# One decoder layer on one core: context rows summed group by group, finished rows through two PSUM banks, their counts one beat later, the last four groups finished on VectorE

## What is computed

```
x = layernorm(x + mamba(x))
x = layernorm(x + slots(x, ctx))
x = layernorm(x + experts(x))

slots: Pn = rmsnorm(ctx); k, v = Pn @ Wk.T, Pn @ Wv.T
       three times:
         q = rmsnorm(s) @ Wq.T
         a = softmax(q k.T / sqrt(128), over the slots), then divided by its sum over the context
         s = gru(a @ v, s)
experts: route = sigmoid(x @ Wr + br); each row goes to its highest expert e
         out = gelu(x @ W1[e]) @ W2[e] * route[e]
```

## Time and profile before

| | us |
|---|---|
| three runs | 1698.12, 1697.04, 1695.10 (median 1697.04) |
| the profiled execution | 1693.93 |
| its span in the trace | 1691.7 |

### The profile page before, as it was taken

How to read it: one execution, slowest core, us unless ns; L and a number is a source line. 1 busy time by engine, 2 the same in 40 slices (tenths; PEclk the granted TensorE clock), 3 DMA queues, 4 the chain that set the end, 5 groups by cost and what they waited for, 6 DMA issues and landing times. The chain is left out here.

```text
span 1691.7 us, 22066 instructions
## 1 busy us (share of the span) xinstructions
PE 1464.0 (87%) x6146; PEld 892.1 (53%) x6146; DVE 1265.3 (75%) x2184; ACT 1098.0 (65%) x2118; POOL 1264.1 (75%) x884
## 2 busy tenths in 40 slices
PE   4988999999998999899987499999999999419994
PEld 1333344343443334343433377777777777319994
DVE  2899999999999999999993267666766767424552
ACT  4778887788878888778864366656656555104553
POOL 2899999999999999999995144567767666643665
PEclk8999999999999999999998599999999999559997
DMA  5355545554555545554542631421470000026771
GB/s 173 135 193 175 168 166 187 181 176 161 195 173 171 180 162 188 186 185 157 170 152 65 204 125 35 152 99 48 149 306 14 7 8 14 7 81 192 210 207 43
DMA packets 126058, 236.92 MB, mean 140 GB/s; under 512 B 13490, under 2 KB 76917, under 8 KB 125952
## 3 DMA queue, kind: packets, MB, share of 16 engines
q1 hardware_dynamic: 121408, 227.21, 41.3%
q0 software_dynamic: 4544, 8.47, 1.5%
HBM read 180.89 MB, written 55.66 MB: 140 GB/s over the span
## 5 line engine op out<-in xcount | busy, mean ns | idle before, releaser
L388 POOL TENSOR_TENSOR hc<-state,c_rows 128x1024 f32<-128x1024 f32 x256 | 599.1, 2361 | 48.7 <-DVE state L585 39.7
L585 DVE TENSOR_TENSOR_SCAN state<-ps_da,inp 128x512 f32<-128x512 f32 x512 | 592.8, 1203 | 29.5 <-ACT ps_da L481 29.5
L704 PE MATMUL ps_y<-hc,ident 128*128 128x512 f32 x1024 | 491.6, 619 | 53.5 <-POOL hc L388 53.5
L481 ACT ACTIVATE ps_da<-dt,a_neg 128x512 f32<-128x512 f32 x512 | 345.3, 688 | 84.6 <-DVE state L585 83.3
L704 PEld LDWEIGHTS ps_y<-hc,ident 128*128 128x128 f32 x1024 | 194.5, 197 | 295.3 <-issue 211.0
L574 DVE TENSOR_TENSOR inp<-dtx,ps_b 128x1024 f32<-128x1024 f32 x192 | 230.4, 1200 | 37.7 <-POOL dtx L359 22.0
L1047 POOL TENSOR_TENSOR rs<-ms,m_half 128x4 f32<-128x4 f32 x48 | 58.8, 1225 | 164.6 <-DVE ms L1223 164.4
L371 POOL TENSOR_TENSOR inp<-dtx,b_rows 128x1024 f32<-128x1024 f32 x64 | 150.9, 2358 | 0.0
L627 PE MATMUL ps_misc<-x1T,w_conv 128*128 128x512 f32 (+3 forms) x256 | 118.8, 609 | 20.1 <-ACT x1T L414 20.1
L487 ACT COPY ps_b<-b_rows 128x512 f32<-128x512 f32 x192 | 111.1, 579 | 38.1 <-DVE inp L574 35.7
L1156 ACT ACTIVATE ex<-sc,nmx,ctx_r 77x128 f32<-77x128 f32 x192 | 92.3, 482 | 40.3 <-DVE nmx L1236 40.3
(11 more groups left out here) (219 smaller groups left out, 2772.6 us busy)
## 6 DMA issues: line engine op xcount, KB each, us to landing
b_rows<-bc_rows SPq DMA_DIRECT2D x128, 512.0 KB, 4.7
c_rows<-bc_rows SPq DMA_DIRECT2D x128, 512.0 KB, 4.0
sorted_x<-pad_rows SPq DMA_DIRECT2D x8, 4160.0 KB, 16.7
w<-in_L_ffn_W SPq DMA_DIRECT2D x78, 256.0 KB
vw<-vw_rows SPq DMA_DIRECT2D x16, 462.0 KB
vw_rows<-vw_out SPq DMA_DIRECT2D x16, 384.0 KB
xrow<-sorted_x SPq DMA_DIRECT2D x39, 130.0 KB, 2.3
x_tok<-in_x SPq DMA_DIRECT2D x16, 256.0 KB, 4.0
```

The lines of the kernel that those rows point to most:

```text
L388: pool.tensor_tensor(hc[:, n % RING], state[:, n % RING], over_c(c_rows[:, slot, n % 2]), ALU.mult).then_inc(hc_ready, 1)
L481: act.activation(ps_da[u % DA_RING][:], dt[:, par, c], ACT.Exp, scale=a_neg[:, c, n:n + 1]).then_inc(da_ready, 1)
L585: dve.tensor_tensor_scan(state[:, n % RING, c], ps_da[u % DA_RING][:], inp[:, n % RING, c], 0.0, ALU.mult, ALU.add).then_inc(state_ready, 1)
L704: ins = pe.matmul(ps_y[:, c], ident[:], hc[:, n % RING, c], start=False, stop=n == NS - 1)
```

## The change

Three things are changed, all in `slot_stage`.

1. **Context.** `root_at` is one beat later for the first four groups and three beats later for the others; ACT sums group 1 at the end of beat 0, group 2 in beat 1, group 3 in beat 2. SP issues the load of group 4 before the clearing, and `kq` of group 3 ahead of `vw` of group 1.
2. **Two banks.** `make_u` writes all four sequences at once, two into `ps_u` and two into `ps_rs`, behind `den_spread`; ACT copies both halves behind its exponentials. `count` moves from the end of beat r+4 to beat r+5, ahead of `root_spread`, which now also waits for ACT's copies. For groups 12 to 15 the counts go to `ps_r`.
3. **The last four groups.** DVE makes their residual, logits and normalised rows; POOL only takes the power (`end_root`), writes labels and scatters. The buffers `row`, `dest_f` and `dest` are doubled, so that groups 14 and 15 have their own and wait for no scatter.

The diff, cut to its core:

```diff
@@ build_program
-        row = [stack.enter_context(nc.sbuf_tensor(f"row{k}", [P, GB, XROW], F32)) for k in range(2)]
+        row = [stack.enter_context(nc.sbuf_tensor(f"row{k}", [P, GB, XROW], F32)) for k in range(4)]
...
@@ slot_stage
+    END = NG - FOUR
+    def kept_row(g):
+        return g % 2 if g < NG - 2 else 2 + g % 2
+    def count_bank(g):
+        return ps_u[:, COUNT_AT:] if g < END else ps_r
     def root_at(g):
-        return g - 1 if g < FOUR else (g // FOUR - 1) * ROUND + ITERS * (g % FOUR) + 1
+        return g if g < FOUR else (g // FOUR - 1) * ROUND + ITERS * (g % FOUR) + 4
     def ctx_parts(n):
-        for g in range(2, NG):
-            if n == max(0, root_at(g) - 2):
+        for g in range(1, NG):
+            if n == root_at(g) - (1 if g < FOUR else 2):
                 yield g, range(0, 2)
-            if n == max(0, root_at(g) - 1):
+            if n == root_at(g) - 1:
                 yield g, range(2, GB)
@@ POOL
+        def end_root(g):
+            k = g % 2
+            pool.wait_ge(end_logits, ev(END_LOGITS, "veps", g - END))
+            pool.tensor_tensor(rstd2[k][:], rstd2[k][:], m_half[:], ALU.pow).then_inc(end_rooted, 1)
...
         def scatter(g):
...
+            if g >= END:
+                hold(pool, end_rows, g - END + 1, passed2[1])
...
-            if g is not None and g < NG - 1:
+            if g is not None and g < END:
                 residual(g)
+            g = post(n, 5)
+            if g is not None and g >= END:
+                labels(g) if g < NG - 2 else last_labels(g)
...
-                logits(g)
+                logits(g) if g < END else end_root(g)
@@ ACT
         def read_u(g, part):
-            act.wait_ge(u_full, 2 * g + part + 1)
-            need(act, rows_done, g - 1)
+            act.wait_ge(u_full, g + 1)
+            need(act, rows_done, min(g - 1, END))
+            need(act, end_rows, g - 1 - END)
+            bank = ps_u if part == 0 else ps_rs
...
-            if g is not None:
-                read_u(g, 0)
             if live(n + 1):
                 square(n + 1)
             if live(n):
                 exps(n)
+            g = post(n, 1)
+            if g is not None:
+                read_u(g, 0)
+                read_u(g, 1)
             if live(n - 2):
                 gate_z(n - 2)
-            if g is not None:
-                read_u(g, 1)
@@ DVE
+        def end_veps(g):
+            dve.tensor_scalar_add(rstd2[k][:], mv2[k][:, :, 1], LN_EPS).then_inc(end_logits, 1)
+        def end_scaled(g):
+            dve.wait_ge(end_rooted, g - END + 1)
+            need(dve, routed, g - 1)
+            dve.tensor_tensor(lg[k][:], tok[k][:, :, P:], over_e(rstd2[k][:]), ALU.mult).then_inc(end_logits, 1)
...
+        def end_norm(g):
+            k, r = g % 2, kept_row(g)
+            if g < NG - 2:
+                dve.wait_ge(scattered[k], 16 * GB * (g // 2))
             for b in range(GB):
...
+            g = post(n, 5)
+            if g is not None:
+                ranks(g)
+                destinations(g)
             g = post(n, 4)
             if g is not None:
                 highest(g)
                 chosen_expert(g)
-                if g >= NG - 2:
-                    last_norm(g)
-            g = post(n, 5)
...
+            g = post(n, 3)
+            if g is not None and g >= END:
+                end_scaled(g)
+                end_norm(g)
+            g = post(n, 2)
+            if g is not None and n >= N:
+                statistics(g)
+                end_veps(g)
@@ PE
         def root_spread(n):
...
+            need(pe, u_read, 2 * made_u[0])
...
                 gate_x(n - 2, 0, ps_r, r_full, True)
+            g = post(n, 5)
+            if g is not None:
+                count(g)
             if live(n):
                 root_spread(n)
...
-                make_u(g, 0)
-            if live(n - 1):
-                den_spread(n - 1)
+                make_u(g, n)
...
-            if g is not None:
-                make_u(g, 1)
-            g = post(n, 4)
-            if g is not None:
-                count(g)
```

More of the change, by code:

```diff
@@ L992, in _ @@
         for g in range(FOUR, RING):
-            load_ctx(g)
+            if g > FOUR:
+                load_ctx(g)
             load_kq(g)
@@ L1119, in _ @@
             g = post(n, 4)
-            if g is not None and g < NG - 2:
+            if g is not None and g < END:
                 normed(g)
@@ L1123, in _ @@
             if g is not None:
-                logits(g)
+                logits(g) if g < END else end_root(g)
             g = post(n, 5)
-            if g is not None:
-                labels(g) if g < NG - 2 else last_labels(g)
+            if g is not None and g < END:
+                labels(g)
             for g in ctx_roots(n):
@@ L1177, in read_u @@
         def read_u(g, part):
-            act.wait_ge(u_full, 2 * g + part + 1)
-            need(act, rows_done, g - 1)
-            act.copy(tok[g % 2][:, 2 * part:2 * part + 2].rearrange("p b d -> p (b d)"), ps_u[:, 0:2 * (P + NE)]).then_inc(u_read, 1)
+            act.wait_ge(u_full, g + 1)
+            need(act, rows_done, min(g - 1, END))
+            need(act, end_rows, g - 1 - END)
+            bank = ps_u if part == 0 else ps_rs
+            act.copy(tok[g % 2][:, 2 * part:2 * part + 2].rearrange("p b d -> p (b d)"), bank[:, 0:2 * (P + NE)]).then_inc(u_read, 1)
         def route_tanh(g):
-            act.wait_ge(logits_made, ev(LOGITS, "logits", g))
+            if g < END:
+                act.wait_ge(logits_made, ev(LOGITS, "logits", g))
+            else:
+                act.wait_ge(end_logits, ev(END_LOGITS, "logits", g - END))
             need(act, choice_made, ev(CHOICE, "less", g - 2))
@@ L1367, in _ @@
             g = post(n, 2)
-            if g is not None:
+            if g is not None and n < N:
                 statistics(g)
+                if g >= END:
+                    end_veps(g)
             if live(n - 3):
```

106 lines of the change are left out of this document (60 added, 46 removed).

## The result

| | before | after | ratio, 95% interval |
|---|---|---|---|
| median, us | 1696.07 (1685.04 to 1698.12, 4 runs) | 1632.31 (1630.92 to 1634.47, 4 runs) | 0.9638 (0.9594 to 0.9682) |
| profiled execution, us | 1693.93 | 1634.47 | |
| its span | 1691.7 | 1632.6 | |
| PE, DVE, POOL, ACT busy | 87, 75, 75, 65% | 88, 78, 77, 67% | |

The kernel became 64 us faster by the medians, 59.5 by the two profiled executions. Those two are compared term by term, since the sum was made against one of them. First the slot stage in four stretches, cut at the first squares row of beats (L1494 now, L1434 before), as in the earlier trace rows. The columns are us, then busy us and instructions of PE, PEld, DVE, ACT and POOL, then the granted clock, the DMA share and GB/s.

A forecast was written before the change was run, and what follows sets the result against it. PE was taken to set 9.18 us beats, with low clock and waits in finishing beats and engines waiting at both ends. Terms 21.1 + 21.4 + 16.2 = 58.7 us off 1697.04 gave 1638, range 1626 to 1657.

The forecast's parts named there:

- Term 1: Start of the slot stage, beats 0 and 1: ACT's wait for group 4's context goes, DVE starts sooner; -21.1 us.
- Term 2: Beats 12 to 46: low clock and waits for `tok` go, some finishing work stays; -21.4 us.
- POOL's late root: Beats 12 to 46: a POOL root following a scatter comes late for PE; 0.3 us for each of 11.
- the first rival: Beats 12 to 46: the low clock stays, 18 us are not gained, 1656 us; chance 0.14.
- Term 3: Last four groups: the last state comes sooner and DVE and POOL finish without waiting for scatters; -16.2 us.
- The start that gives less: Start of the slot stage: context rows or a `vw` load late, 15 of 21 us lost, 1653 us; chance 0.04.
- the slower case: Beats 12 to 46: PE falls to the low clock for good, 1758 us if all 35 are low; chance 0.02.
- The rival of the end: End of the slot stage: POOL's four roots wait for DVE, ten of 16 us go, 1648 us; chance 0.12.

The follow-up runs named there:

- another execution: Kernel before with own row, dest_f and dest buffers for groups 14 and 15; beats 12 to 46 took 360.36 us, the profiled execution 1680.39 us.
- a later run: Kernel after with the scatters of groups 12 and 13 issued one beat sooner on POOL: 1627.42 us, ratio 0.9595 to before.

## Why the prediction was right, and where it was not

The prediction said 1638 and faster; the time is 1632.31, inside its range. By the profiled executions it said 1635.2 and got 1634.47, so most of the 5.7 us by which the medians differ from it is how the profiled executions stand to their medians: before's lay below its median by 2 to 3 us, after's lies above by 2.2.

**Term 1 was right** in size and mechanism: -20.7 for -21.1. The copy of the scores came at 932.03 (931.1 forecast, in a stage that itself began 1.3 us later), and PE's spread root, not the copy, set DVE's start, as said. Beat 1 ended at 938.28, forecast 936.6; without the 1.3 the difference is 0.4. Nothing was late next: behind the stage's first loads, which the change leaves alone, no load is waited for. By its letter the text's own test (ACT nowhere waits over 1 us for context) fails, for ACT waits 3.33 us for the first group's rows, as it did before. Group 4's place in the queue, from which the text explained the stall, is worth nothing once the sums have their new beats; with the old beats the new queue is worth 13.4.

**Term 2 was right in its mechanism and too small in size.** The waits and the low clock are gone in the changed kernel; the three beats take 10.25, 9.82 and 9.19 (10.4, 9.9 and 9.3 forecast). The mis-sized terms are what is left: 26.0 forecast, 342.78 - 35 x 9.18 = 21.5 measured. A half of `make_u` was costed with the duration of its row, 0.63, where the next row of PE starts 0.47 later: the twelve beats with `make_u` last 13.5 us longer than 9.18 each, instead of 15.1, the eleven with a count 7.3 (7.6 forecast), the others 0.7. And POOL's late root was given 3.3 us: in the profile of after PE has no wait for `rs` at all, and where other executions have it, it is 1.5 us at most. The low clock itself was put at 18.4 by the rounded mean of 0.95; by the beats it was 16.6.

**The clock was forecast rightly with a reason that does not hold as put,** so that hit is in part luck. The text tied the low clock to the count's waits. The counts in their old place fit that (0.43 us of wait, clock 0.98), though three of eleven beats behind such a wait had the low clock and eight had not; but the doubled counts had the low clock with no wait at all. The rule of the Trainium skill (TensorE: Matmul & The Clock Gate, Part 1), that the low clock is the state after idleness, does not describe these stretches either: in the window at 1228.00 PE was busy 6.00 of 6.00 us at a clock of 0.72. What the rule was taken to mean for this change, that the low stretches stay, did not happen: the first rival (1656) is out. Its other half, that a wait of 1 us is not the whole cause, the doubled counts bear out. And the clock's part of term 2 is itself one draw: the same code took 8.3 us less in another execution.

**Term 3 was too large by 3.1 us, in one of its pieces.** From the residual to the last variance DVE took 14.95 us (15.7 forecast), POOL from its last root to its last label 14.5 (14.6), and the last state came 3.05 sooner (3). The stage ended 34.4 us behind the last residual where the text had some 31. What failed is "with 1.0 to the next stage": it took 4.92, 3.9 more, of which 0.75 came back on DVE. The row for it was in the earlier trace rows all along, the idle time of 4.92 behind POOL's queue at 1500.42. It was read as POOL waiting for others, since DVE's last row in that trace ended only 1.05 us ahead of it. But when POOL is last the 4.92 are on the path, and POOL was made last. The text also said that idle times of POOL over 3 us there would show the term wrong. There are two, 3.88 and 4.50, and yet the pieces up to POOL's last label came out: the forecast's own sum had POOL's rest start behind DVE's last variance, so it held these idle times already. That test was badly chosen; that the idle time could be used was the finding of a later run.

The other rule of the Trainium skill (SBUF — State Buffer, SBUF: two separate sides), by which a DVE instruction with two SBUF inputs and a POOL instruction that reads SBUF run one after the other, would have made the end 2.9 us later by stretching the eight DMAs of the two scatters. From POOL's last root on they fit the forecast without it (14.5 for 14.6). A little of it may show ahead of that, from POOL's side, though no run isolates it: beside DVE's instructions with two inputs in SBUF, the issues of a scatter take 1.09 and 1.20 us, at 1406.64 and 1408.03, and 0.96 for the fourth at 1409.54; `keep` and `mix` of DVE beside them stay at 0.68 and 0.69.

**The rivals.** The start that gives less is refuted by the 20.7, the slower case by the clock of 1.00. That case was also priced wrongly: the beat of 12.6 us is not one with the low clock throughout. The window of beat 31 in the kernel before (columns as above) has a mean clock of 0.73, between the two levels, so a beat wholly at the low one would take longer.

```profile
1251.53:1264.14 12.61, 12.40 (x65) 9.48 (x64) 7.15 (x23) 5.49 (x14) 6.44 (x11) 0.73 0.75 301
```

The rival of the end had the right sign and the wrong mechanism: it put 10 us on hand-overs from DVE to POOL, but these pieces took what the forecast gave them, and the end gave 3.1 less through the stage's end.

## What to carry to other kernels

Cost a matmul by the start of the next row of PE, not by its duration, and read idle time ahead of a stage's first instruction as a price of the engine that you are about to make the last one. If an engine waits for a load, ask in which beat it uses it before you reorder the queue: with the use two beats later, a load that had cost 15 us of waiting was early from either place. Where the granted clock is under 1.00, take several executions before a term is built on it.

## What the runs showed of the hardware

- The low clock of PE came in a stretch in which PE was busy throughout: a mean of 0.72 over 6.00 us, behind doubled counts, and rows of 1.10, 0.66 and 1.06 us took 1.57, 1.09 and 1.86. It came in four of eleven beats with the same instructions, so it isn't set by the program's order alone, and at DMA shares from 0.00 to 0.81.
- A stage that POOL ended with labels behind indirect DMAs took 4.92 us from POOL's last row to the next stage, in twelve traces; a stage that POOL ended with a memset, without such DMAs, 0.31.
- One half of `make_u`, two f32 matmuls of 136 columns (x4 in a row of PE), cost 0.47 us of PE's time where the row says 0.63.
